# Weighing the values in two halves, one of them in the half-step of the maxima

## What is computed

```
q, k, v = heads(x @ Wq + bq), heads(c @ Wk + bk), heads(c @ Wv + bv)   # 16 heads of 16
scores  = einsum('bhqd,bhkd->bhqk', q, k)            # self: * 1/4, + bias, future masked
w       = softmax(scores, axis=-1)
x       = layernorm(x + einsum('bhqk,bhkd->bhqd', w, v).merge_heads() @ Wo + bo)
```

## Time and profile before

| | us |
|---|---|
| median of 3 runs | 1757.24 |
| lowest, highest | 1756.34, 1758.70 |
| the profiled execution's own time | 1757.24 |
| its span, first to last instruction | 1755.5 |
| TensorE busy in the span | 1487.1 |
| VectorE busy | 1050.9 |
| ScalarE busy | 972.5 |
| GpSimd busy | 632.7 |
| mean granted TensorE clock | 0.927 of full |

### The profile page before, as it was taken

The page is one execution under the profiler, slowest core; times in us unless marked ns, Lnnn a source line. Parts: engine busy times, 40 slices in busy tenths (PEclk is TensorE's granted clock), DMA queues, the critical chain, the costliest instruction groups (busy, mean ns, idle before and its releaser), DMA issues. The chain is left out here.

```text
span 1755.5 us, 43097 instructions
## 1 busy us (share of the span) xinstructions
PE 1487.1 (85%) x17640; PEld 1218.8 (69%) x17640; DVE 1050.9 (60%) x2275; ACT 972.5 (55%) x1419; POOL 632.7 (36%) x615
## 2 busy tenths in 40 slices
PE   5999999999999999999998492223999999999950
PEld 4777777777777777777777441222999999999950
DVE  3666666666666767676767347795544544455425
ACT  3666666666676766666676320012755655555517
POOL 1544444444442223232221000045344545454326
PEclk9999999999999999999999795555999999999985
DMA  5011111121111222222221251003344434442239
GB/s 189 21 56 56 56 56 56 51 61 44 57 49 62 74 74 74 74 74 74 74 62 38 91 158 12 0 0 93 82 90 96 101 49 87 96 101 44 26 51 356
DMA packets 129793, 130.10 MB, mean 74 GB/s; under 512 B 28288, under 2 KB 116464, under 8 KB 129472
## 3 DMA queue, kind: packets, MB, share of 16 engines
q1 hardware_dynamic: 114496, 106.88, 19.9%
q0 software_dynamic: 15104, 20.48, 7.4%
HBM read 83.13 MB, written 44.20 MB: 73 GB/s over the span
## 5 line engine op out<-in xcount | busy, mean ns | idle before, releaser
L489 ACT ACTIVATE at_pr<-at_A 128x2048 f32<-128x2048 f32 x128 | 240.7, 1880 | 202.7 <-PE at_A L319 202.7
L581 DVE TENSOR_REDUCE at_mx<-at_A 128x12 f32<-128x1536 f32 x128 | 224.6, 1754 | 58.9 <-PE at_A L286 56.8
L34 PE MATMUL ex_D<-ex_w,ex_hT 128*128 128x256 f32 (+1 forms) x1920 | 233.8, 281 | 0.4
L34 PEld LDWEIGHTS ex_D<-ex_w,ex_hT 128*128 128x128 f32 (+1 forms) x1920 | 230.5, 184 | 3.1 <-DVE ex_raw L1418 1.9
L34 PE MATMUL ex_U<-ex_xT,ex_w 128*128 128x384 f32 (+1 forms) x1152 | 223.1, 353 | 0.0
L708 POOL TENSOR_SCALAR_AFFINE_SELECT at_pr<-at_pr 128x2048 f32<-128x2048 f32 x64 | 128.5, 2008 | 246.9 <-ACT at_pr L489 246.9
L1474 POOL DMA_INDIRECT total<-ex_o,ex_ids x80 | 131.6, 1645 | 228.8 <-DVE ex_o L1423 197.1
L34 PEld LDWEIGHTS ex_U<-ex_xT,ex_w 128*128 128x128 f32 x1152 | 208.1, 190 | 7.4
L1408 DVE TENSOR_TENSOR ex_hT<-ex_h,ex_hT 128x384 fp32r<-128x384 f32 (+1 forms) x192 | 112.6, 586 | 98.0 <-ACT ex_hT L1368 87.4
L617 DVE TENSOR_TENSOR at_oT<-at_C,at_oT 128x512 fp32r<-128x512 f32 x64 | 44.2, 691 | 175.9 <-ACT at_oT L502 175.9
L319 PE MATMUL at_A<-at_qp,at_kt 32*128 32x256 f32 x2048 | 141.1, 390 | 0.0
(11 more groups left out here) (185 smaller groups left out, 2714.3 us busy)
## 6 DMA issues: line engine op xcount, KB each, us to landing
ex_w_in<-in_w SPq DMA_DIRECT2D x16, 1024.0 KB
at_turned<-in_x_turned SPq DMA_DIRECT2D x16, 512.0 KB, 4.1
at_x<-in_x SPq DMA_DIRECT2D x16, 512.0 KB, 3.8
x<-at_y SPq DMA_DIRECT2D x32, 256.0 KB, 2.2
at_x<-x SPq DMA_DIRECT2D x16, 512.0 KB, 3.7
at_turned<-in_ctx_turned SPq DMA_DIRECT2D x16, 512.0 KB, 4.2
rows<-at_y SPq DMA_DIRECT2D x32, 256.0 KB, 2.2
total<-at_y SPq DMA_DIRECT2D x32, 256.0 KB, 2.8
```

The source lines that it names most:

```text
L34: last = nc.tensor.matmul(out, pick_l(left, a), pick_r(right, b), start=(start and n == 0), stop=(stop and n == 2))
L489: nc.scalar.activation(pr[:, k % 2].rearrange("p i n a q -> p (i n a q)"), A[:].rearrange("p i n a q -> p (i n a q)"), ACT.Exp).then_inc(e ...
L581: nc.vector.tensor_reduce(mx[:, k % 2, 0:12], A[:, 0:3].rearrange("p i n a k -> p (i n a) k"), AX, ALU.max).then_inc(max_done, 1)
```

## The change

The weighing is cut in two: `weigh(k, n)` does the 16 matmuls of one sequence. Half 0 of set k-1 stays where the weighing was, behind `scores(k)`. Half 1 of set k-2 comes in the half-step of the maxima, directly behind `maxima(k+1)`, and waits until `take_max(k)` has copied mT. `set_back(k-2)` moves from ahead of the step's projection or output to behind it, directly ahead of the scores. The transposed maxima go to the second half of C[0], columns G and on of the bank seen as bf16, and so wait for an older copy of o. On ScalarE, `copy_o(k-2)` stands behind `copy_bank(k+1)`, where `copy_o(k-1)` stood behind `exps(k)`. The first maxima come ahead of the first two v projections, and the order at the end of the stage follows the new halves.

```diff
--- before.py
+++ after.py
@@ -290,11 +290,11 @@
 
             def turn_max(k):
                 pe.wait_ge(m2_ready, k + 1)
-                if k >= 2:
-                    pe.wait_ge(o_copied, k - 1)
+                if k >= 3:
+                    pe.wait_ge(o_copied, k - 2)
                 b = C[0][:, :].bitcast(BF16)
                 for n in range(2):
-                    last = nc.tensor.matmul(b[:, n * P:(n + 1) * P], m2[:, k % 2, n, :], ident_b[:],
+                    last = nc.tensor.matmul(b[:, G + n * P:G + (n + 1) * P], m2[:, k % 2, n, :], ident_b[:],
                                             start=True, stop=True, is_transpose=True)
                 last.then_inc(mt_full, 1)
 
@@ -320,22 +320,25 @@
                                                 start=False, stop=(n == 1), skip_group_check=True)
                 last.then_inc(score_full, 1)
 
-            def weigh(k):
+            def weigh(k, n):
 
                 g, np_, half = k // 4, k // 2 % 2, k % 2
-                pe.wait_ge(exp_done if cross(g) else sel_done, k + 1)
-                pe.wait_ge(v_done, 2 * g + np_ + 1)
-                pe.wait_ge(mt_done, min(k + 2, sets))
-                if k == sets - 1:
-                    pe.wait_ge(o_copied, k)
+                if n == 0:
+                    pe.wait_ge(exp_done if cross(g) else sel_done, k + 1)
+                    pe.wait_ge(v_done, 2 * g + np_ + 1)
+                    pe.wait_ge(mt_done, min(k + 2, sets))
+                    wait(pe, o_copied, k)
+                else:
+                    pe.wait_ge(mt_done, min(k + 3, sets))
                 b = C[0]
-                for n in range(2):
-                    for quad in range(2):
-                        for j in range(4):
-                            last = nc.tensor.matmul(b[32 * j:32 * j + VW, (2 * n + quad) * P:(2 * n + quad + 1) * P],
-                                                    v[:, g % 2, 2 * np_ + n, half * HEADS_HALF + 4 * quad + j, :],
-                                                    pr[:, k % 2, 2 * quad + j // 2, n, j % 2, :], start=True, stop=True)
-                last.then_inc(o_full, 1)
+                for quad in range(2):
+                    for j in range(4):
+                        last = nc.tensor.matmul(b[32 * j:32 * j + VW, (2 * n + quad) * P:(2 * n + quad + 1) * P],
+                                                v[:, g % 2, 2 * np_ + n, half * HEADS_HALF + 4 * quad + j, :],
+                                                pr[:, k % 2, 2 * quad + j // 2, n, j % 2, :], start=True, stop=True,
+                                                skip_group_check=True)
+                if n == 1:
+                    last.then_inc(o_full, 1)
 
             def set_back(k):
 
@@ -387,11 +390,11 @@
             project_k(0, 0)
             project_q(0, 1)
             project_k(0, 1)
+            pe.wait_ge(tables_ready, 1)
+            maxima(0)
             project_v(0, 0)
             project_v(0, 1)
-            pe.wait_ge(tables_ready, 1)
             pe.wait_ge(v_ready, 1)
-            maxima(0)
             for k in range(sets):
                 g, s = divmod(k, 4)
                 more = g + 1 < groups
@@ -400,7 +403,7 @@
                 if k + 1 < sets:
                     maxima(k + 1)
                 if k >= 2:
-                    set_back(k - 2)
+                    weigh(k - 2, 1)
                 if s == 0:
                     if more and cross(g + 1):
                         turn_x(g + 1, 1)
@@ -413,9 +416,12 @@
                 elif s == 3 and more:
                     project_v(g + 1, 0)
 
+                if k >= 2:
+                    set_back(k - 2)
+
                 scores(k)
                 if k >= 1:
-                    weigh(k - 1)
+                    weigh(k - 1, 0)
                 if k % 2 == 1 and k >= 3:
                     output_back((k - 3) // 2)
                 if more:
@@ -429,8 +435,10 @@
                         project_v(g + 1, 1)
                         if g + 2 < groups and cross(g + 2):
                             turn_x(g + 2, 0)
-            weigh(sets - 1)
+            weigh(sets - 2, 1)
             set_back(sets - 2)
+            weigh(sets - 1, 0)
+            weigh(sets - 1, 1)
             output(halves_of - 2)
             set_back(sets - 1)
             output_back(halves_of - 1)
@@ -523,6 +531,8 @@
                 more = g + 1 < groups
                 if k + 1 < sets:
                     copy_bank(k + 1)
+                if k >= 2:
+                    copy_o(k - 2)
                 if s == 0 and more and cross(g + 1):
                     if g + 1 == layer_groups:
                         act.wait_ge(made, 1)
@@ -532,8 +542,6 @@
                 elif s == 3 and more and not cross(g + 1):
                     take_v(g + 1, 0)
                 exps(k)
-                if k >= 1:
-                    copy_o(k - 1)
                 if k % 2 == 1 and k >= 3:
                     copy_out((k - 3) // 2)
                 if s == 0 and more:
@@ -553,6 +561,7 @@
                     normalise(2 * g - 2)
                 elif s == 3 and g >= 1:
                     normalise(2 * g - 1)
+            copy_o(sets - 2)
             copy_o(sets - 1)
             copy_out(halves_of - 1)
             normalise(halves_of - 2)
@@ -595,7 +604,7 @@
                 if k >= 2:
                     dve.wait_ge(score_full, k - 1)
                 nc.vector.tensor_copy(mT[:, k % 2].rearrange("p n q -> p (n q)"),
-                                      C[0][:, :].bitcast(BF16)[:, 0:2 * P]).then_inc(mt_done, 1)
+                                      C[0][:, :].bitcast(BF16)[:, G:G + 2 * P]).then_inc(mt_done, 1)
 
             def normalise_set(k):
                 u, half = divmod(k, 2)
```

## The result

The changed kernel takes 1815.84 us (median of 4 runs, 1814.65 to 1816.24) against 1756.79 for the kernel before in the same series (4 runs). The ratio is 1.0336, 95% interval 1.0318 to 1.0354: slower by 59 us. The profiled execution has a span of 1814.5 us against 1755.5, so the profile shows the same 59.0 us.

A forecast was written before the change was run, and what follows sets the result against it. Self was taken as bounded by TensorE's own stream, cross by waits standing in it. Losses of 13.1 us in self and 32.6 in cross, 45.7 together on 1757.2, gave 1803 us, with a range of 1778 to 1816.

The forecast's parts named there:

- main case: Whole kernel: the change makes it slower, 1803 us, with bounds 1786 to 1815 including the stage ends; chance 0.64.
- rival D: Split costs over 0.25 us, or a ScalarE queue delays the exponentials: each 0.1 us a set is 13 us; 1820, chance 0.09.
- Self has nothing to win, 13.1 us to lose: Self layer: TensorE never waits; 64 x 0.15 for shape changes plus 15 x 0.23 waiting for the copy of o.
- c: Cost a set of one more change of the array's shape on TensorE, taken as 0.15 us, between 0 and 0.25.
- Cross, step 0, +1.00: Second half of the weighing waits for mT behind the rest of the turned x: +1.00 us a group, largest term.
- Cross, step 2, +0.47: Turn back waits for ScalarE's copy of o behind the bank's copy, so scores start later: +0.47 us a group.
- Cross, steps 1 and 3, +0.35 each: New wait of 0.20 us for the mT copy, 0.35 us each with the shape change.
- The clock: TensorE's granted clock, 1.00 in both windows, was to stay at full; no cost put on it.
- The ends, 0 with a bound of 3: Start and end of the stage: shifts of 0.5 to 2 us of both signs, taken as 0, bound 3 us.
- A: Faster: the shift evens out cross and new waits don't bind, if mT is copied early enough; 1746 us, chance 0.08.
- B: No difference: new waits replace old ones in cross, loads hide self's extra block; 1757 give or take 3, chance 0.07.
- C: Turn back doesn't bind and the split is free, only the mT waits left: 19 us, 1776, chance 0.12.

The follow-up runs named there:

- the one with the old head: The changed kernel with the first maxima behind the first two v projections again: 1813.68 us.
- the last kernel tried: Kernel before with out copied ahead of o (cross step 3), normalising behind the bank copy, first x turn behind the next maxima: 1756.3 us.

## Why the prediction was right, and where it was off

The direction and the two main mechanisms, the wait for mT in step 0 and the queue of ScalarE, were right and in the right place. The time was 13 us short. It lies above the 1815 that the bounds of the main case gave, and inside the stated range by 0.2 us only: the range had been stretched to 1816 for a dearer split or delayed exponentials (rival D), and neither happened. What filled the gap, the clock, the longer ends and GpSimd, had been put at nothing or nearly so. That the range held is luck.

- *Self has nothing to win, 13.1 us to lose.* A steady group costs 0.75 us, against 4 x 0.15 + 0.23 = 0.83 predicted. The wait in step 0 is 0.20 (0.23 predicted), and c is 0.14 on average, but not evenly: 0.09, 0.17, 0.06 and 0.24 in steps 1, 2, 3 and 0. The 0.16 that I read for entering the full shape from column strips isn't one: behind half a weighing the same projection takes 1.50 us, not 1.64. What costs is one more block of strips, as the experiment with a third block shows.
- *Cross, step 0, +1.00.* Measured +0.85 at full clock: the x turn 0.49 earlier (0.47 said), the new wait until 2.23 us after it (2.31 said).
- *Cross, step 2, +0.47.* Measured +0.55, by the queue named: moving the normalising takes 0.57 away.
- *Cross, steps 1 and 3, +0.35 each.* Step 3 has +0.17, of which some 0.1 is the wait for mT, where I had 0.20 and a larger c. The short waits for mT that the profile lists, 15 of 0.39 us, are not in these steps, as I had said they would be, but in step 2, where `rest_o` stands ahead of the copy. Step 1 has +0.59. It holds a cost that I had excluded. I had the q projection's input ready in time and GpSimd's list unchanged; but the addition of bo follows the second x turn, which now comes later, and so meets VectorE's cast of the maxima. VectorE's timeline of the changed kernel at that place:

```profile
724.26 1.48 DVE L598 CAST at_m<-at_mx 128x16 bf16<-128x16 f32 x1
```

and GpSimd's:

```profile
723.33 2.38 POOL L712 TENSOR_TENSOR at_x<-at_x,at_bo 128x1024 f32<-128x1024 f32 x1 [1.63 <-PE at_B L208]
```

The cast, 175 ns by itself, lasts 1.48 us and ends when the addition does (723.33 + 2.38 = 725.71). Each group at full clock loses 0.4 us at the q projection. That the sum of the four steps is 2.16 us, with 2.17 predicted, is luck: steps 0 and 3 were put too high, steps 1 and 2 too low, and it cancels.

- *The clock.* This is the step that failed: "nothing in the change makes the stage idle enough for me to change that". The windows around the x turn of another group (columns as in the earlier trace rows, the number ahead of the DMA share is the granted clock):

```profile
753.00:754.00 1.00, 0.00 (x0) 0.00 (x0) 0.88 (x3) 1.00 (x4) 0.75 (x1) 1.00 0.00 0
754.00:755.00 1.00, 0.93 (x17) 0.55 (x18) 1.00 (x2) 0.56 (x3) 0.00 (x0) 0.67 0.01 5
755.00:756.00 1.00, 1.00 (x5) 1.00 (x6) 1.00 (x2) 0.58 (x1) 0.00 (x0) 0.50 1.02 329
756.00:757.00 1.00, 1.00 (x6) 1.00 (x6) 0.96 (x2) 0.59 (x1) 0.92 (x1) 0.50 1.07 256
757.00:758.00 1.00, 1.00 (x8) 1.00 (x7) 1.00 (x1) 0.00 (x0) 1.00 (x1) 0.63 0.90 307
```

and TensorE's timeline there:

```profile
754.07 0.88 PE L336 MATMUL at_C<-at_pr,at_v 128*32 128x128 f32 x16 [1.14 <-DVE at_mT L606]
...
755.65 2.61 PE L34 MATMUL at_B<-at_wo,at_oT 128*128 128x256 f32 x12
```

TensorE had idled 1.3 us for v and then, after 1.1 us of work, 1.1 us for mT; at 754 the clock falls to 0.50, its lower level of 1.2 GHz, and stays there for some 3.5 us. The output (755.65) takes 2.45 us to the next block instead of 1.52. There are eight such stretches between 520 and 1000 us, none in the cross groups of the kernel before, where the clock is low only from 989 us on, at the end of the stage. The step takes about 12.0 us instead of 10.48. Over the 15 groups that is 39.7 - 15 x 2.16 = 7 us net (a slow step spares the next one the meeting with GpSimd), and some 1.1 net in the step ahead of set 64. The experiments bear it out: with the wait for mT gone there is no such stretch, with it, alone or in the change, there is.
- *The ends, 0 with a bound of 3.* They cost 5 us: 2.5 at the head, where the copy of the bank stands behind the split of the source (the cast there too lasts 1.21 us, beside GpSimd's subtraction) and the low clock lasts longer, and 2.5 at the tail. Both had been seen and taken as 0. The tail is the last copy of o behind a normalising, as the prediction names it: TensorE waits 2.21 us for it, and moving the normalising takes 2.5 us away.
- *The rivals.* A, the gain, would have needed the mT copy ahead of the rest of the turned x. With it the kernel is at 1788, so A's price was too high even with its condition met: the queue and the split remain. B fell: the new waits came on top of the old one. C fell: the turn back did bind, in step 2 of cross and step 0 of self, and the split cost 0.14 us a set in self. Of D, the split stayed under 0.25 us a set and no queue of ScalarE held the exponentials up in every set. Its price was also added up wrongly: 13 us on 1803 are 1816, not 1820.

The share of each term, as it was taken away one behind the other: wait for mT with its clock 27.6 us, queue of ScalarE 12.3 (15.8 when it was taken away first), GpSimd's addition and the head together 8.4 (0.42 x 15 = 6.3 of it the addition, once the clock is full), split and the rest 10.

## What to carry to other kernels

A block that moves ahead in an in-order queue takes its waits with it, and everything behind it inherits them: list what it waits for at its new place, and what stands ahead of that on the other engine. Cover is worth nothing where the bound is an engine's own stream, so a balancing of half-steps has to be read against the step in which an engine really waits. Of such a change, try the part that frees a queue alone: here it gave 6 us, and with a neighbour 12, without the split.

## What the runs showed of the hardware

- Two idle stretches of TensorE of 1.3 and 1.1 us with 1.1 us of work between them brought the granted clock from 1.00 to 0.50 for about 3.5 us, in eight of the 15 such places between 520 and 1000 us of the changed kernel. Of the other kernels with both stretches, the one with the wait alone had this three times and the one with the old head nine times; with 1.3 and 0.56 us it came four times. With one stretch alone it came at none of these places: not with 1.4 us in the kernel before, not with 1.3 us when the mT copy was first, not with 1.5 us in the last kernel tried. What decides between two equal groups is not settled by these runs.
- A cast of 16 elements a partition on VectorE, 175 ns alone, took 1.5 to 2.4 us in the 15 cross groups of the changed kernel while a tensor_tensor of GpSimd ran on SBUF. GpSimd's instruction had started first each time, and the cast ended 0.03 us behind it. With the addition moved away the mean fell from 627 to 176 ns. The Trainium skill, SBUF — State Buffer, § SBUF: two separate sides, says that VectorE and GpSimd share a pair of ports as an exclusive lock: of a GpSimd instruction and a VectorE one in a two-port mode, the one that starts first holds it for its whole length, and the other one waits. The trace agrees with that for this cast; in which mode the cast ran, no trace shows.
- One more block of column strips between blocks of the full array cost 0.24 us with the same matmuls, about 0.1 us for each of its two changes of shape. The Trainium skill, TensorEngine Tiling (Array Packing), § Tiling Modes, says that a change of the tiling mode drains TensorE; the trace agrees in kind, with a cost each time, and the page gives no price to compare it with.
